# Graph attention kernel: 80 chunks instead of 70 take their projected rows from the matmul walk, with 8 blocks beside each of the first 45 chunks

## The reference

```python
h_proj = jnp.einsum('nd,rde->rne', h, relation_weight)      # 32 relations
t_r = h_proj[etype, src]
h_r = h_proj[etype, dst]
att = jnp.sum(t_r * jnp.tanh(h_r + efeat), axis=-1)
seg_max = segment_max(att, dst); att_exp = jnp.exp(att - seg_max[dst])
a = att_exp / segment_sum(att_exp, dst)[dst]
h_nb = segment_sum(h[src] * a[:, None], dst)
out = leaky_relu((h + h_nb) @ res_w1.T) + leaky_relu(h * h_nb @ res_w2.T)
x = layernorm(x + out)
```

## Time and profile before

| | |
|---|---|
| median of 3 runs | 10518.47 us |
| the profiled execution | 10518.84 us, of which span 10517.0 us |
| setup | 0 to 491 us |
| far chunks: first and last sum with edge features | 554.8 and 4049.8 us |
| near chunks: first and last such sum | 4103.7 and 6263.3 us |
| nodes of layer 1, all of layer 2 | 6290 us to the end |
| busy over the whole span | PE 31%, DVE 45%, ACT 25%, POOL 74% |

### The profile page before, as it was taken

One profiled execution on the slowest core, in us unless ns is written; L12 is line 12 of the kernel. 1 busy time (PEld: TensorE's weight loads), 2 busy tenths in 40 slices (PEclk: granted clock), 3 DMA queues, 4 the chain that ended last, 5 costly groups with the idle time before them and its releaser, 6 DMA issues. The chain is left out here.

```text
span 10517.0 us, 77420 instructions
## 1 busy us (share of the span) xinstructions
PE 3213.4 (31%) x16334; PEld 2868.5 (27%) x16500; DVE 4729.7 (45%) x5151; ACT 2635.5 (25%) x2314; POOL 7749.0 (74%) x8165
## 2 busy tenths in 40 slices
PE   5567777777777774000000013000000000000001
PEld 2256766667676764000000003000000000000001
DVE  4455555555555556778777775111111111111113
ACT  3212222222222222222222224222222222222221
POOL 3677777777777777777777765777777777777776
PEclk8755555555555555555555555555555555555555
DMA  9967777777777776444444441111111111111111
GB/s 364 322 164 181 180 182 179 178 180 181 178 183 181 180 180 162 137 128 132 134 128 137 128 115 42 52 51 54 51 54 51 51 54 51 54 51 54 51 51 52
DMA packets 1330242, 1325.37 MB, mean 126 GB/s; under 512 B 1053304, under 2 KB 1099288, under 8 KB 1317130
## 3 DMA queue, kind: packets, MB, share of 16 engines
q1 hardware_dynamic: 1038169, 748.56, 27.8%
q0 software_dynamic: 254688, 368.09, 15.0%
q10 hardware_dynamic: 37344, 208.28, 5.1%
HBM read 781.03 MB, written 543.26 MB: 126 GB/s over the span
## 5 line engine op out<-in xcount | busy, mean ns | idle before, releaser
L1204 POOL DMA_INDIRECT gs<-table,idx_s x3125 | 3008.2, 963 | 994.1 <-issue 974.2
L1568 POOL DMA_INDIRECT gy<-ytab,idx x3125 | 2951.6, 945 | 1011.3 <-issue 951.8
L1512 PEld LDWEIGHTS banks<-win,pick 128*125 128x125 f32 x9900 | 2150.7, 332 | 338.2 <-issue 312.7
L1512 PE MATMUL banks<-win,pick 128*125 (+1 forms) x9900 | 2121.1, 413 | 186.8 <-DVE pick L1260 185.7
L1603 DVE TENSOR_TENSOR_SCAN run<-keep,add 128x1664 f32<-128x1664 f32 (+1 forms) x126 | 453.2, 3597 | 3016.4 <-ACT add L1633 3016.4
L1208 POOL DMA_INDIRECT gd<-table,idx_d x1375 | 1363.7, 992 | 419.0 <-issue 419.0
L540 PE MATMUL ps_cm<-tail,mask_m 128*128 128x64 f32 x196 | 43.6, 423 | 4007.2 <-DVE mask_m L475 4007.2
L540 PEld LDWEIGHTS ps_cm<-tail,mask_m 128*128 128x128 f32 x196 | 42.3, 331 | 4008.5 <-DVE mask_m L475 4008.5
L1633 ACT COPY add<-gy 128x1600 f32<-128x1600 f32 (+1 forms) x126 | 400.8, 3181 | 2353.8 <-DMA gy<-ytab,idx 2353.8
L1496 PE MATMUL banks<-hi,lo 128*128 128x98 bf16 x3125 | 278.8, 283 | 2004.4 <-DVE hi L1247 2004.4
L1496 PEld LDWEIGHTS banks<-hi,lo 128*128 128x128 bf16 x3125 | 263.9, 145 | 2019.3 <-DVE hi L1247 2019.3
(11 more groups left out here) (263 smaller groups left out, 4671.8 us busy)
## 6 DMA issues: line engine op xcount, KB each, us to landing
proj_d<-found SPq DMA_DIRECT2D x330, 512.0 KB
win<-table SPq DMA_DIRECT2D x660, 240.0 KB
table<-rows SPq DMA_DIRECT2D x98, 1536.0 KB, 8.8
sums<-rowbuf ACTq DMA_DIRECT2D x124, 825.0 KB
ef<-in_edge_attr_dram SPq DMA_DIRECT2D x125, 800.0 KB, 4.5
sums<-rowbuf ACTq DMA_DIRECT2D x124, 800.0 KB, 3.5
keyb<-step_keys SPq DMA_DIRECT2D x332, 234.4 KB, 5.5
gd<-proj_d SPq DMA_DIRECT2D x70, 800.0 KB, 5.9
```

Source lines behind the costliest of these rows:

```text
L1204: pool.indirect_dma_start(out=gs[:, s, g, :], out_offset=None, in_=table_vec, in_offset=bass.IndirectOffsetOnAxis(ap=idx_s[:, s, g:g + 1], ...
L1512: nc.tensor.matmul(acc[k][0:MT, bass.ds(slots[t] * D, D)], pick[:, w, t * MT:(t + 1) * MT], win[:, w, bass.ds(at_w, 1), :].rearrange("p o ...
L1568: pool.indirect_dma_start(out=gy[:, s, g, :], out_offset=None, in_=ytab, in_offset=bass.IndirectOffsetOnAxis(ap=idx[:, s, g:g + 1], axis=0 ...
```

## The change

FAR goes from 55 to 45: 45 chunks gather their `h_r` rows, 80 take them from the walk. The walk has 8 blocks beside each of the 45, 360 in all instead of 330. `win` and `pick` have two buffers instead of three, so a window is issued, and a pick made, once block b-2 is done. DVE's eight picks stand at new places: four together after `front`, then one each after the sum, the exponentials' arguments, `edge_rows` and the one-hots. ACT's copies move with them: three ahead of the copy of `gs`, and three after the store. In the setup, one array (`node_high`) shares memory with another, one search step moves by a table block, and the lists get longer (43 columns of steps instead of 39, 16 tiles to a partition instead of 14). The 16 numbers of `pe_tab` are loaded at the head of each block as before.

```diff
-FAR = 55
+FAR = 45
-PER = 6
+PER = 8
-KSLOTS, WSLOTS = 4, 3
+KSLOTS, WSLOTS = 4, 2
...
-            node_high = sb(c1, "node_high", [P, TILE_OF, NB], BF16)
+            node_high = kk[:, :, :].rearrange("p u e -> p (u e)")[:, TILE_OF * P // 2:TILE_OF * (P + NB) // 2].bitcast(BF16).rearrange("p (k j) -> p k j", j=NB)
...
-                    for q, (n0, n1) in enumerate(((17, 18), (18, 19), (19, 20), (20, 22), (22, 23)), 1):
+                    for q, (n0, n1) in enumerate(((17, 18), (18, 20), (20, 21), (21, 22), (22, 23)), 1):
...
                     def front(c, s, i, link, far=False):
-                        if far:
-                            picks(c, s, i, 0)
...
                         if far:
-                            picks(c, s, i, 1)
+                            for j in range(4):
+                                picks(c, s, i, j)
...
                         if far:
-                            picks(c, s, i, 2)
+                            picks(c, s, i, 4)
...
                         link.then(nc.vector.copy_predicated(vec[:, :, 0, :], mask, prod[:, t0:t1, :]))
-                        if far:
-                            picks(c, s, i, 3)
...
                         if far:
-                            picks(c, s, i, 4)
+                            picks(c, s, i, 5)
...
                         if far:
-                            picks(c, s, i, 5)
+                            picks(c, s, i, 6)
                         if go_on:
                             low_hots(c + 1, link)
                             high_hots()
+                        if far:
+                            picks(c, s, i, 7)
...
                             take_found(PER * c, 0)
+                            take_found(PER * c + 1, 1)
...
                         if far:
-                            take_found(PER * c + 1, 1)
+                            take_found(PER * c + 2, 0)
...
                         if far:
-                            take_found(PER * c + 2, 0)
+                            take_found(PER * c + 3, 1)
...
                         if far:
-                            take_found(PER * c + 3, 1)
                             take_found(PER * c + 4, 0)
+                            take_found(PER * c + 5, 1)
+                            take_found(PER * c + 6, 0)
```

## The result

The changed kernel takes **10745.36 us** (median of 3 runs, 10742.66 to 10748.01): 1.0216 times the time before, 95% interval 1.0199 to 1.0233. The forecast was 10750. The profiled execution has a span of 10746.2 us, 229.2 more than before.

What follows compares the result with a forecast made beforehand. PE was to bound far chunks: 66.2 + 5.0 + 3.0 + 3.0 = 77.2 us. Far stage -98, its end +10, near stage +313, setup +3 make +228, so 10750 us; range 10620 to 10900.

Steps and rivals of the forecast that it cites:

- PE takes POOL's place: Far chunks: PE, at 77.2 us a chunk, becomes the bound instead of POOL with its 64.7 us of gathers.
- The first rival: Far chunks: POOL stays the bound at 64.7 us, 10187 us in all, given a higher clock or shorter load; chance 4%.
- eight undisturbed blocks: PE's far period: eight blocks of 8.28 us each, 66.2 us, already more than POOL's 64.7.
- histogram and the load behind it: PE's far period: from block 5's head to block 0's takes 13.29 us, adding 5.0 over 8.28.
- the late copy: ACT's copy of block 4, awaited by block 5's last matmul, comes 1.8 us late; with a longer load, plus 3.0.
- longer register loads: PE's block heads: SP's window issues lengthen the load by 0.5 us in each of six blocks, plus 3.0 a chunk.
- The check at the prediction's end: Sign of a wrong forecast: the period is right but register loads still have a median of 3.95 us.
- POOL idle by some 12 us a chunk: Far chunks, expected sign: POOL waits about 12 us a chunk for DVE's row numbers.
- Windows in time: Window DMAs with two buffers: landing takes 6.6 us, needed after 9.2, so 2.6 to spare and cost 0.
- Shares: Far chunks: DMA engines busy 61.4 of 77.2 us, 0.80; PE busy 67 of 77 us at clock 0.50.
- this rival: POOL staying the bound because denser blocks let PE's clock go from 1.2 to 2.4 GHz; POOL rival's chance 4%.
- the rest is behind the table's stores: Setup: beyond +2.6 us for `step_keys` with 43 columns instead of 39, nothing else delays the start; +3 in all.

Runs made afterwards that it cites:

- e7: Changed kernel with each block's 16 bytes loaded as 8 two-byte numbers and taken apart on PE; 10484.19 us, ratio 0.9966.
- e13: Kernel before the change, with the 16 numbers loaded as 8 pairs; 10522.99 us, ratio 0.9991.
- e5b: Kernel before the change, with the 16 numbers loaded a second time at each block's head, both sets used; 11495.11 us, one run.
- e9: Changed kernel with ACT's copy of block 4 ahead of the result's copy, and the 16 bytes loaded as 4 words, unpacked on PE; 10222.84 us, ratio 0.9704.
- e1: Changed kernel with ACT's copy of block 4 moved ahead of the copy of the chunk's result; 10593.56 us, ratio 1.0069.
- e12: Changed kernel with the setup's search step put back at its old place; 10743.26 us, ratio 1.0205.
- e14: As e9, with the setup's search step also put back at its old place; 10165.80 us, ratio 0.9668.

## Why the prediction was right

The bound and the mechanism were right. The period came out right in part by luck, since sizes inside it were off and made up for each other, and the step for the setup failed.

**The bound.** The step "PE takes POOL's place" is shown from both sides: the register load halved gives 5.9 us a period in the changed kernel (e7) and nothing before (e13); doubled, it costs 17.2 us a period even before (e5b). The first rival, POOL as the bound, named its own condition, a shorter load, and e9 shows that the condition was the right one: with loads of 0.33 us the period is 65.12.

**The terms of 77.2**, with what the runs say:

| term | forecast | measured |
|---|---|---|
| eight undisturbed blocks | 66.2 | 8 x 8.28 = 66.2; four in each chunk are at it |
| histogram and the load behind it | 5.0 | 13.38 - 8.28 = 5.1 |
| the late copy | 3.0 | 3.4 (77.04 - 73.66, e1), of which 2.8 the later start of the load and 0.5 a longer load |
| longer register loads | 3.0 | 2.3 (the remainder; in e1 the excess of blocks 5 and 6) |

The last is right as a sum and wrong in its place. The prediction gave each of six blocks 0.5 us, since a window's issue falls on each load. The trace shows no such rule: a load at whose end the window's issue begins is 3.79 to 3.88 us in the mean, undisturbed. Three loads in each chunk are long, those into which SP and ACT issue several DMAs: block 0's, 5's and 6's, 4.95, 4.71 and 5.64 us in the median. Those of blocks 5 and 6 cost 1.0 and 1.3 us (in e1). That of block 0 lies in the row of the histogram, where 1.2 of the 5.1 us are its excess; before it was as long (4.86 us), so the 5.0 taken over from there had it inside. The kernel before, with three buffers, had three long loads in a chunk too (4.86, 4.86 and 5.97 us), so it need not be the two buffers that make them. The check at the prediction's end, that the loads' median must rise above 3.95, came out against it (3.81): five loads in eight are clean now, and three in six were.

**The copy of block 4** was forecast by following DVE's chain: copy at e+33.9 with 1.8 us of lateness. In the chunk shown, e (the end of block 1) is 2493.1; the copy ends at 2526.4, e+33.3. The time of the copy holds to 0.6 us. Its lateness doesn't: the four blocks passed in 34.1 us, not in 35.2, and the load behind the copy starts 2.8 us later than undisturbed, not 1.8. The load's own excess by it is 0.5 instead of 1.2, so that the sum of 3.0 came close.

**POOL idle by some 12 us a chunk**: 12.6. **Windows in time**: yes, 2.5 us of waiting in the whole kernel. The 6.6 us taken for a landing were low beside the landing that e9 shows, 8.0 us (2396.77 to 2404.77, with the DMA engines busier); of the 9.2 us there were to land in, 1.2 would remain by that.

**Shares.** The DMA engines were to be at 0.80 and are at 0.73. PE was to be busy 67 of 77 us and is 64 (2730 us in 620 to 3900): a block's matmuls are 7.6 us, as e9 shows, not 8.1.

**The clock.** With eight denser blocks the granted clock stayed at 0.50. In e9, with PE busy 10.00 of 10 us (2410 to 2420), it still read 0.50, but see the last section. The Trainium skill ("TensorE: Matmul & The Clock Gate", What's actually happening), which says that activity releases the throttle, stood for this rival; in the blocks of this kernel the trace doesn't agree, and the measurement decides.

**The setup** is where a step failed: "the rest is behind the table's stores". `step_keys` was issued 13.4 us later and landed 28.4 instead of 25.8 us after. The 2.6 were forecast. The 13.4 were not: e12 returns them with the one moved search step (issue at 462.4), so the longer lists cost next to nothing at the start (first sum 555.4 against 554.8). The working priced the longer lists and put the moved search step at nothing. The size scatters: the seven other kernels with the step at its new place have their first sum at 562.9 to 569.5 us, so the 16.0 measured here are its dear end. That the total still came out within 5 us is luck: the far stage was 7 better, the near one 3 and the rest 2, against 13.

## What to carry to other kernels

A number that an engine loads into a register is work in that engine's own stream, and a busy share doesn't count it. Before giving an engine more blocks, take the distance of two undisturbed blocks (here 8.28 us), not their busy time, times the new count; and if the product comes near the bound, look first for what can be taken out of the stream. Then follow the one strictly ordered engine that serves the loop (here ACT) through the new period; a single instruction behind a long one cost 3.4 us of 77. The waits of the profile don't show such a wait when it falls in the stream of instructions; the idle time is put down to "issue". And before a wait is called a cost, follow what its releaser stood behind: the wait for a window in e9 is one for POOL.

## What the runs showed of the hardware

- Register loads on PE from SBUF: 16 numbers of one byte 3.79 us, 8 of two bytes 1.92, 8 of one byte 1.92, 4 of four bytes 0.33. So 0.24 us a number from 8 to 16 of them, but 0.08 for the four words; whether that is the count of four or the width of the words was not separated.
- A load in whose time SP or ACT issue DMAs is longer. In the changed kernel (700 to 3300 us) loads of 16 numbers with one such issue begun in them took 3.79 to 4.22 us, with three or four 4.5 to 5.4, with five 5.4 to 6.2; in e7 the 8 pairs took 1.92 to 1.95 with none or one and 2.6 to 4.3 with two to five. No run varied this by itself. The longest are 7.95 us for 16 numbers, 4.89 for 8 pairs and 0.93 for 4 words (e14). Two loads back to back (e5b): the second takes 4.8 us in the median.
- PE's clock in e9, by stretch (us, PE busy, PEld, DVE, ACT, POOL, clock, DMA share, GB/s):

```profile
2434.50:2436.60 2.10, 2.10 (x28) 2.10 (x28) 1.76 (x1) 1.01 (x1) 1.49 (x3) 0.50 0.20 51
2436.60:2437.40 0.80, 0.80 (x6) 0.49 (x4) 0.35 (x1) 0.00 (x0) 0.77 (x1) 0.59 0.87 201
2437.40:2439.00 1.60, 1.58 (x15) 1.45 (x13) 0.00 (x0) 0.00 (x0) 1.02 (x2) 1.00 1.35 221
2439.00:2441.00 2.00, 1.93 (x11) 1.41 (x10) 0.00 (x0) 0.00 (x0) 1.70 (x2) 0.92 1.02 303
2441.00:2443.00 2.00, 2.00 (x11) 2.00 (x12) 0.00 (x0) 0.00 (x0) 1.39 (x3) 0.50 0.54 174
```

PE is hardly ever idle here (8.41 of 8.50 us busy). The first stretch is the histogram, 25 short bf16 matmuls; right behind it the clock rises to 2.4 GHz, and it falls to 1.2 again in the middle of the next block, with PE busy throughout. In the kernel before such a rise fell into the open register load, where it is worth nothing; in the chunk of the changed kernel shown above there was none behind the histogram. From 500 to 3500 us every rise starts 1.7 to 4.8 us after the start of a histogram, in each of the ten kernels looked at: in the changed kernel in 9 of 39 chunks, where PE then stands idle for an open register load, and in e9 in 42 of 46, where the block follows at once. Over the far stage the mean is 0.54 in e9 and 0.51 in the changed kernel. With the short load the block gets it: 15 matmuls in 1.6 us against 11 in 2.0, and from the end of block 7 to the end of block 0, histogram included, 8.5 us in the mean where 7.6 + 2.0 would be 9.6. A block of fp32 walk steps never raised the clock here, with PE busy for 22.90 of 22.90 us (2411.60 to 2434.50) at 0.50; what in the histogram does was not tested.
